# Layer 3's norm: the joining of the statistics on GpSimd, and the copy of x behind the root

## The chip, the core and the metric

The kernel runs on one core of a Trainium2 chip. The metric is the device time of one execution in microseconds (us), median of several runs. Engines are named as in the profile: PE (TensorE; PEld is its weight load), DVE (VectorE), ACT (ScalarE), POOL (GpSimd), SP (SyncE, which issues most DMAs).

## The reference

Four graph layers run one after the other over 16 batches of 512 nodes by 128 features. Each adds its result to x and is followed by a layer norm. The change is in the last layer (a graph attention with one head) and its norm:

```
m = mean(x); v = var(x); norm(x) = (x - m) / sqrt(v + eps)

Wh = x @ W;  s1 = Wh @ a1;  s2 = Wh @ a2
e = leaky_relu(s1[:, :, None] + s2[:, None, :])
e = where(adj == 0, -inf, e)
x = norm(x + softmax(e) @ Wh)
```

## The kernel before

Layer 3 works through 16 batches, b = 0 to 15. A batch is 512 nodes, held as four tiles of 128 nodes on the partitions. Every engine has its own hand-written list of items for one step; in `k:n` the item k works in step s on batch s − n. So PE, ACT and DVE work on several batches in one step, and each engine goes through its list strictly in order, waiting at semaphores.

- **PE** (L1447 to L1510) per step: `w0 q2 w1 q3 a3 i x a0 j a1 q0 q1 a2`. Item `x` transposes batch s from its copy `Xc` (L1458) and waits for that copy. `j` (L1477) makes the row terms s2 of the same batch, from the transposed x that ACT has copied out (`xTr`, L1322). `a0`, `a1`, `a2` (and `a3` one step later) multiply the exponentials `pr` by `Wh` (L1496) for batch s − 2. `w` (L1468), `q` (L1507, L1508) and `i` (L1484) are the other products.
- **DVE** per step: `m0 m1 d0 e0 e1 r0 m2 e2 e3 m3 r1 d1 c0 c1 r2 r3 b B`. The four `m` (L1377) take the row maxima of batch s and need its `j`. `e` (L1385) forms the scores of batch s − 1 and needs its `q`. For batch s − 2, `d` (L1401) and `r` (L1409) divide the product by its row sum and add x into the tile `rc`; `d1` needs `a3`. `b` takes the statistics of the norm (L142, four instructions: mean and sum of squares of the two halves of 128 features). `B` joins the halves (`bn_aggr`, L148, four instructions).
- **POOL** per step s, from s = 4 on (`pool_rest`, L1298): the copy of batch s into `Xc` (`pool_copy`, L1270 to L1275), then for batch s − 3 the root (L155 adds eps, L157 raises to −0.5), then the application, four instructions that write `rc` in place (L183). The first four copies and the norm of batch 0 are made ahead of that loop, so twelve copies (batches 4 to 15) are made in it.
- **SP** stores `rc` to memory when the application is done (L1243). Tiles `rc` exist twice, so `r` of batch b waits for the store of batch b − 2.

What sets the order around the change are these lists and the semaphores. The twelve copies stand in POOL's list in front of the root of batch s − 3, and thus right behind the application of batch s − 4. The norm of the last two batches ends differently: DVE applies it (`dve_last`, L1418 to L1437).

Of the kernel before, what the change touches and what calls it, by code (L numbers as in the profile page):

```python
# [23 lines left out]
ALU = mybir.AluOpType  # L24
# [3 lines left out]
P = 128  # L28
B, N, D = 16, 512, 128
NT = N // P  # L30
# [5 lines left out]
EPS = 1e-5  # L36
MASKED = -1.0e30
CREDIT = 2
# [3 lines left out]
def after(b, per, k=None):  # L42

    return (b + CREDIT) * per + (per if k is None else k)


def hold(eng, gate):


    eng.sem_inc(gate, 1)  # L50
# [136 lines left out]
def layer0(nc, m, ins, bank, L1):  # L187
# [3 lines left out]
    with ExitStack() as own:  # L191
# [112 lines left out]
        def order(text):  # L304
# [22 lines left out]
        }  # L327
        LAST = {
            "PE": order("#w0 #a0 p p p p #a1 #h0 p p p p #v0"),
# [814 lines left out]
def staged(text):  # L1144

    return [(word.split(":")[0], int(word.split(":")[1])) for word in text.split()]


def layer3(nc, own, m, bank, out, rl1_at, ready):
# [6 lines left out]
    def over(name, shape, dt=F32):  # L1156
        words = 1
        for n in shape[1:]:
            words *= n
        t = nc.alloc_sbuf_tensor_at(name, shape, dt, offset=at[0])  # L1160
        at[0] += -(-words * (2 if dt == BF16 else 4) // 32) * 32
        return t

    def sem(name):
        return own.enter_context(nc.semaphore("c_" + name))
# [11 lines left out]
    mx = [over(f"mx3{k}", [P, NT]) for k in range(2)]  # L1177
    em = [over(f"em{k}", [P, 2, NT]) for k in range(2)]
    rec = [over(f"rec3{k}", [P, NT]) for k in range(2)]
    at[0] = 205120  # L1180
    pr = [over(f"pr{k}", [P, NT, N]) for k in range(2)]
    norm = Norm(nc, own, m, "n3")
# [4 lines left out]
    x_f = sem("x_copied")  # L1187
# [9 lines left out]
    rcp = sem("reciprocal")  # L1197
    res = sem("residual")
    stored = [sem(f"stored{k}") for k in range(2)]
    last_eps, last_rstd, last_x, last_stored = (sem(f"last_{x}") for x in ("eps", "rstd", "applied", "stored"))  # L1200
    gate = sem("gate")
    LAST = B - 1
    out_bank = [bank[6], bank[7]]

    PE_ORDER = staged("w0:1 q2:2 w1:1 q3:2 a3:3 i:1 x:0 a0:2 j:0 a1:2 q0:1 q1:1 a2:2")
    ACT_ORDER = staged("L3:2 E0:2 W0:1 W1:1 E1:2 XR:0 G:1 L0:1 L1:1 X:0 L2:1")
    DVE_ORDER = staged("m0:0 m1:0 d0:2 e0:1 e1:1 r0:2 m2:0 e2:1 e3:1 m3:0 r1:2 d1:2 c0:0 c1:0 r2:2 r3:2 b:2 B:2")

    def is_batch(b, n):
        return isinstance(b, int) and b == n  # L1210
# [22 lines left out]
    third = Memory()  # L1233

    def sync(sp):
# [9 lines left out]

        pairs(sp, LAST - 1, 1, step)
        step(LAST - 1, 0, [True], LAST // 2)
        sp.wait_ge(last_x, 2)
# [12 lines left out]
    def pool_constants(pool):  # L1261
        pool.sem_inc(x_f, CREDIT)
        norm.credit_pool(pool)
        norm.credit_apply(pool)
        pool.wait_ge(*ready["O"])
        for n, ap in enumerate((onesb[:], Wh[0][:, :, 0:1], Wh[1][:, :, 0:1])):
            pool.memset(ap, 1.0).then_inc(const, 1)

    def pool_copy(pool, s, par, first=False):
        pool.wait_ge(x_ps, after(s - 2, 1))  # L1270
        pool.wait_ge(ready["X"], after(s, 4))
        if not first:
            pool.wait_ge(norm.s_x, after(s - 4, 4))
        hold(pool, gate)
        pool.tensor_copy(flat(Xf[par][:]), batch_flat(m.X, s)).then_inc(x_f, 1)  # L1275

    def pool_last_root(pool):
        rstd, aggr = norm.rstd[1], norm.aggr[1]
        pool.wait_ge(norm.s_x, after(LAST - 2, 4))
        for h in range(2):  # L1280
            two = slice(2 * h, 2 * h + 2)
            pool.wait_ge(norm.s_aggr, after(LAST, 4, 2 * h + 2))
            hold(pool, gate)
            pool.tensor_scalar(rstd[:, two], aggr[:, two, 1], EPS, 1.0, ALU.add, ALU.mult).then_inc(last_eps, 1)
            pool.wait_ge(last_eps, h + 1)
            pool.tensor_tensor(rstd[:, two], rstd[:, two], m.neg_half[:, 0:2], ALU.pow).then_inc(last_rstd, 1)

    def pool_norm(pool, b, par, copied):
        pool.wait_ge(x_f, after(copied, 1))
        if isinstance(b, int) and b == LAST:  # L1290
            pool_last_root(pool)
            return
        norm.root(pool, b + CREDIT, par)
        if isinstance(b, int) and b == LAST - 1:
            return
        norm.apply(pool, b + CREDIT, par, r[par], lambda k: r[par][:, k])

    def pool_rest(pool):  # L1298

        def step(s, par, alive, nth):  # L1300
            if alive[0]:
                pool_copy(pool, s, par)
            pool_norm(pool, s - 3, 1 - par, s if alive[0] else B - 1)

        pairs(pool, B, 4, step, first=4)

# [62 lines left out]
    def dve_items(dve):  # L1369

        def item(name, b, par, nth):
            what, k = name[0], int(name[1]) if name[-1].isdigit() else 0
            if what == "m":
                dve.wait_ge(s2_ps, after(b, 1))
                dve.wait_ge(s_mx, after(b, NT, k - 1))
                hold(dve, gate)
                dve.tensor_tensor_reduce(out=junk[k % 2][:], in0=s2_bank(b)[:], in1=m.mask_ij[:, k],  # L1377
                                         scale=1.0, scalar=3.0 * MASKED, op0=ALU.add, op1=ALU.max,
                                         accum_out=mx[par][:, k:k + 1]).then_inc(s_mx, 1)
            elif what == "e":  # L1380
                if k == 0:
                    dve.wait_ge(av, after(b - 2, NT))
                dve.wait_ge(relu, after(b, NT, k + 1))
                dve.wait_ge(r_ps, after(b, NT, k + 1))
                dve.scalar_tensor_tensor(out=pr[par][:, k], in0=bank[4 + k % 2][:],  # L1385
                                         scalar=Wh[par][:, k, S2_SLOPE:S2_SLOPE + 1], in1=rl[par][:, k],
                                         op0=ALU.add, op1=ALU.add).then_inc(e_s, 1)
            elif name == "c0":
                dve.wait_ge(s_mx, after(b, NT))
                dve.wait_ge(wh_c, after(b, 2))  # L1390
                dve.scalar_tensor_tensor(out=em[par][:, 0], in0=Wh[par][:, :, S1], scalar=SLOPE - 1.0, in1=mx[par][:],
                                         op0=ALU.mult, op1=ALU.subtract).then_inc(e_m, 1)
            elif name == "c1":
                dve.wait_ge(e_m, after(b, 2, 1))
                dve.wait_ge(d_g, after(b - 2, NT))
                dve.scalar_tensor_tensor(out=em[par][:, 1], in0=mx[par][:], scalar=-SLOPE, in1=em[par][:, 0],
                                         op0=ALU.mult, op1=ALU.min).then_inc(e_m, 1)
            elif what == "d":
                dve.wait_ge(av, after(b, NT, 2 * k + 2))
                dve.wait_ge(res, after(b - 2, NT))  # L1400
                dve.reciprocal(rec[par][:, 2 * k:2 * k + 2],  # L1401
                               out_bank[k][:, 0:2 * (D + 2)].rearrange("p (t d) -> p t d", t=2)[:, :, 0]
                               ).then_inc(rcp, 1)
            elif what == "r":
                h, t = divmod(k, 2)
                if t == 0:
                    dve.wait_ge(rcp, after(b, 2, h + 1))
                    dve.wait_ge(stored[par], (nth + 1) * 16)
                dve.scalar_tensor_tensor(out=r[par][:, k], in0=out_bank[h][:, t * (D + 2) + 1:t * (D + 2) + D + 1],  # L1409
                                         scalar=rec[par][:, k:k + 1], in1=tile_of(m.X, b, k),  # L1410
                                         op0=ALU.mult, op1=ALU.add).then_inc(res, 1)
            elif what == "b":
                dve.wait_ge(res, after(b, NT))
                norm.statistics(dve, b + CREDIT, par, r[par])
            elif what == "B":
                norm.aggregate(dve, b + CREDIT, par)

        return item  # L1418

# [101 lines left out]
def layers2_3(nc, m, bank, wide, out, L1):  # L1521
# [4 lines left out]
    with ExitStack() as own:  # L1526
# [3 lines left out]
        def sem(name):  # L1530
            return own.enter_context(nc.semaphore(name))
# [15 lines left out]
                 for h in range(2)] + late,  # L1547
# [8 lines left out]
        norm = Norm(nc, own, m, "n2")  # L1556

        bn = sem("bn_applied"); b_ps = sem("bn_turned"); res1 = sem("residual1")
        x_f = sem("x_in_place")
# [13 lines left out]
        gate = sem("gate")  # L1573
        agg = sem("bn2_aggregated"); root = sem("bn2_root"); aff = sem("bn2_factors")
        STACKED = 3 * 16
        third = layer3(nc, own, m, bank, out, qkT_at,
                       {"O": (bn, after(B - 1, 1)), "X": norm.s_x, "score banks": (s_mx, after(B - 1, TILES)),
                        "second wide": (t_exp, after(B - 1, EXPS)), "first two": (t_exp, after(B - 1, EXPS, EXPS - 1)),
                        "ring": ((rcp, after(B - 1, 1)), (o_n, after(B - 1, 1)))})
# [4 lines left out]
        DVE_ORDER = staged("ql:3 b:7 u3:4 kl:3 u0:3 R:0 c1:6 u1:3 B:0 c2:6 u2:3")  # L1584
# [73 lines left out]
        def _(pool):  # L1658
# [41 lines left out]
            third.pool_copy(pool, 2, 0, first=True)  # L1700
            third.pool_copy(pool, 3, 1, first=True)
            tail("r.15 g2.15", POOL_ORDER, work, None)
            third.pool_norm(pool, 0, 0, 3)
            third.pool_rest(pool)

        @block.scalar
# [311 lines left out]
```

## Time and profile before

| what | value |
|---|---|
| median of 3 runs | 933.6 us (933.47 to 933.91) |
| the profiled execution, device time | 933.39 us |
| its span, first to last instruction | 931.6 us |
| layer 3 in it | from about 795 us to the end |
| PE / DVE / ACT / POOL busy, 847.6 to 864.8 us (two steps, 17.2 us) | 16.57 / 15.83 / 14.35 / 9.94 us |

The difference between device time and span, 1.8 us, lies around the profile's first and last instruction. The views used are the table of busy time by stretch, the chain of waits (followed back from the last instruction and given in order of time), and the timeline (merged instructions in order of time; in brackets the engine's idle time just before, and what ended it).

### The profile page before, as it was taken

What the parts mean: (1) busy time and instruction counts of PE and PEld (TensorE: products, weight loads), DVE (VectorE), ACT (ScalarE), POOL (GpSimd) and SP (SyncE); (2) the same over time, 40 slices, a digit from 0 to 9 for tenths busy, and PEclk for the clock granted to TensorE, in tenths of its full rate; (3) what the DMA queues carried; (4) which work ended last, traced back from release to release, by engine and by line L of the source; (5) the groups of instructions that cost most, each with busy time, mean ns of one, the idle gap of its engine ahead of it and who ended that gap; (6) DMA issues with size and microseconds to landing.
All of it is one profiled execution on the core that took longest, in us unless ns stands there. A gap on an engine that the chain in (4) does not pass through costs nothing. (4 is left out here: it accounts for less than half of the span.)

```text
span 931.6 us, 20358 instructions
## 1 busy us (share of the span) xinstructions
PE 864.7 (93%) x6039; PEld 619.7 (67%) x6039; DVE 624.1 (67%) x1931; ACT 506.6 (54%) x903; POOL 404.0 (43%) x451
## 2 busy tenths in 40 slices
PE   6999999999999999977679999999999998999996
PEld 4799999999999998843344444444444444777775
DVE  4756645545545556467676887778876652899997
ACT  4332221211211236566457787888877667888884
POOL 4010211211111225300435788887887776456554
PEclk9999999999999999999979999999999999999999
DMA  9100000000010000000133443333433430010111
GB/s 253 35 9 15 13 12 12 24 12 13 23 30 4 13 1 0 0 0 1 34 70 69 87 102 86 68 78 81 99 82 69 87 86 1 13 34 23 34 34 45
DMA packets 34249, 40.82 MB, mean 44 GB/s; under 512 B 6673, under 2 KB 17553, under 8 KB 34193
## 3 DMA queue, kind: packets, MB, share of 16 engines
q1 hardware_dynamic: 32816, 39.87, 17.9%
q8 instruction: 28, 0.46, 0.2%
q10 hardware_dynamic: 1376, 0.27, 0.1%
q14 instruction: 29, 0.23, 0.1%
HBM read 6.43 MB, written 4.19 MB: 11 GB/s over the span
## 5 line engine op out<-in xcount | busy, mean ns | idle before, releaser
L1686 POOL TENSOR_TENSOR half_sum<-prob 128x1024 f32<-128x1024 f32 x64 | 151.4, 2378 | 21.3 <-PE bank L1950 18.4
L1761 ACT ACTIVATE prob<-wide 128x1024 f32<-128x1024 f32 x128 | 124.1, 1022 | 38.4 <-PE wide L1942 38.1
L460 ACT CAST yT<-wide 128x512 fp32r<-128x512 f32 x48 | 28.1, 589 | 190.8 <-PE wide L870 141.9
L1830 DVE CUSTOM_DVE_ANT_0 junk<-wide,mask_ij 128x512 bf16<-128x512 f32 x128 | 82.8, 684 | 51.2 <-PE bank L1922 50.7
L1938 PE MATMUL wide<-qk_st 128*128 128x512 f32 x256 | 84.5, 437 | 4.9 <-ACT prob L1761 3.3
L1830 DVE CUSTOM_DVE_ANT_0 junk<-bank,mask_ij 128x512 bf16<-128x512 f32 x128 | 83.0, 686 | 0.0
L553 POOL TENSOR_TENSOR Xr<-Xf,Xr 128x512 fp32r<-128x512 f32 x16 | 20.4, 1293 | 140.1 <-ACT Xr L455 139.9
L1496 PEld LDWEIGHTS bank<-Wh,pr 128*128 128x128 f32 x512 | 65.2, 191 | 14.0 <-ACT pr L1349 6.5
L1496 PE MATMUL bank<-Wh,pr 128*128 128x129 f32 x512 | 68.5, 278 | 4.8 <-ACT pr L1349 4.2
L59 PE MATMUL bank<-z,L3T_hi 128*128 128x256 f32 x256 | 72.4, 283 | 0.4 <-DVE z L678 0.4
L61 PE MATMUL bank<-z,L3T_lo 128*128 128x256 f32 x256 | 72.3, 283 | 0.0
L60 PE MATMUL bank<-z,L3T_hi 128*128 128x256 f32 x256 | 72.3, 282 | 0.0
L1938 PEld LDWEIGHTS wide<-qk_st 128*128 128x128 f32 x256 | 46.6, 194 | 32.4 <-DVE mx L1830 18.5
L155 POOL TENSOR_SCALAR n_rstd<-n_aggr 128x4 f32<-128x4 f32 x31 | 6.3, 204 | 129.1 <-DVE n_aggr L148 123.7
L1960 PE MATMUL bank<-prob,v 128*32 128x512 f32 x512 | 61.4, 598 | 0.2 <-ACT prob L1761 0.2
L664 DVE TENSOR_TENSOR yT<-wide,yT 128x512 fp32r<-128x512 f32 x48 | 32.9, 686 | 31.8 <-ACT yT L460 31.8
L687 DVE TENSOR_TENSOR zf<-bank,G 128x256 f32<-128x256 f32 x64 | 27.0, 421 | 34.6 <-PE bank L61 33.1
L59 PEld LDWEIGHTS bank<-z,L3T_hi 128*128 128x128 f32 x256 | 48.8, 191 | 2.0 <-DVE z L678 1.2
L60 PEld LDWEIGHTS bank<-z,L3T_hi 128*128 128x128 f32 x256 | 48.8, 191 | 0.4
L1922 PEld LDWEIGHTS wide<-qkT 32*128 32x128 f32 x128 | 12.3, 184 | 55.2 <-ACT prob L1761 29.2
L61 PEld LDWEIGHTS bank<-z,L3T_lo 128*128 128x128 f32 x256 | 48.9, 191 | 0.0
L558 POOL TENSOR_TENSOR Xa<-X,Xa 128x512 fp32r<-128x512 f32 x16 | 20.6, 1293 | 59.8 <-ACT Xa L429 59.8
(302 smaller groups left out, 2392.0 us busy)
## 6 DMA issues: line engine op xcount, KB each, us to landing
qk_st<-qkT SPq DMA_DIRECT2D x192, 128.0 KB, 2.4
out_dram<-rc SPq DMA_DIRECT2D x15, 256.0 KB, 2.3
Xf<-X SPq DMA_DIRECT2D x14, 256.0 KB, 2.3
A<-in_adj_dram SPq DMA_DIRECT2D x4, 256.0 KB, 5.0
qk_st<-neg_row SPq DMA_DIRECT2D x64, 2.0 KB
Xf<-in_x_dram SPq DMA_DIRECT2D x2, 256.0 KB, 7.0
mask_q<-mask_ji SPq DMA_DIRECT2D x16, 32.0 KB, 1.8
w<-in_L_gnn_W_dram SPq DMA_DIRECT2D x2, 128.0 KB, 2.2
```

The source lines that it names most:

```text
L59: pe.matmul(out, stat[0], mov[0], start=start, stop=False)
L60: pe.matmul(out, stat[0], mov[1], start=False, stop=False)
L61: return pe.matmul(out, stat[1], mov[0], start=False, stop=stop)
L460: act.copy(yT[bb][i][0][:], psum_y[i][:]).then_inc(y_hi, 1)
L664: dve.tensor_tensor(yT[bb][i][1][:], psum_y[i][:], yT[bb][i][0][:].bitcast(F32), ALU.subtract).then_inc(y_lo, 1)
L687: dve.tensor_tensor(zf[:, t], psum_h[k % 2][:, 0:GB * D], G[1 - par][:, 1 if k < NT else 0, t], ALU.add).then_inc(h_sb, 1)
L1496: last = pe.matmul(out_bank[h][:, t * (D + 2):t * (D + 2) + D + 1], pr[par][:, j, k * P:k * P + P], Wh[par][:, j, 0:D + 1], start=(j == 0) ...
L1686: pool.tensor_tensor(flat(half_sum[h][:]), flat(prob[bp][h][:, 0:2]), flat(prob[bp][h][:, 2:4]), ALU.add).then_inc(h_sum, 1)
L1761: act.activation(flat(prob[bp][h][:, 2 * half:2 * half + 2]), wide[half][:], ACT.Exp, scale=SCALE).then_inc(t_exp, 1)
L1830: dve.tensor_tensor_reduce(out=junk[h % 2][:], in0=ROWS[h][:], in1=m.mask_ij[:, i], scale=1.0, scalar=3.0 * MASKED, op0=ALU.add, op1=ALU.m ...
L1938: pe.matmul(bank[j][:], k_st[:, k, j * P:j * P + P], q_st[:, k], start=True, stop=True)
L1960: last = pe.matmul(ring["V0"][c, :], v[bp][:, k, c], prob[bp][h][:, k], start=(k == 0), stop=(k == NT - 1), skip_group_check=True)
```

## The change

POOL, not DVE, now joins the halves of the statistics. DVE's item `B` is gone. In its place POOL has `pool_root`: eight instructions on 128x4 operands (difference, sum and square of the means, sum of squares and their scaling), with semaphore waits on its own earlier results, and then the power as before. The copy of batch s, which stood in front of the root of batch s − 3, stands behind it and ahead of the application. The last batch keeps `bn_aggr` on DVE.

```diff
-    DVE_ORDER = staged("m0:0 ... c1:0 r2:2 r3:2 b:2 B:2")
+    DVE_ORDER = staged("m0:0 ... c1:0 r2:2 r3:2 b:2")
...
+    def pool_root(pool, b, par):
+        stats, aggr, rstd, w = norm.stats[par], norm.aggr[par], norm.rstd[par], terms[par]
+        means, sums = (stats[:, :, 1], stats[:, :, 4]), (stats[:, :, 2], stats[:, :, 5])
+        pool.wait_ge(norm.s_stats, after(b, 4))
+        pool.wait_ge(norm.s_x, after(b - 2, 4))
+        hold(pool, gate)
+        pool.tensor_tensor(w[:, 0], means[0], means[1], ALU.subtract).then_inc(s_joined, 1)
+        pool.tensor_tensor(w[:, 1], means[0], means[1], ALU.add).then_inc(s_joined, 1)
+        pool.tensor_tensor(w[:, 2], sums[0], sums[1], ALU.add).then_inc(s_joined, 1)
+        pool.wait_ge(s_joined, after(b, JOINED, 1))
+        pool.tensor_tensor(w[:, 3], w[:, 0], w[:, 0], ALU.mult).then_inc(s_joined, 1)
+        pool.wait_ge(s_joined, after(b, JOINED, 3))
+        hold(pool, gate)
+        pool.tensor_scalar(aggr[:, :, 0], w[:, 1], 0.5, 1.0, ALU.mult, ALU.mult).then_inc(s_joined, 1)
+        pool.tensor_scalar(w[:, 2], w[:, 2], 1.0 / D, EPS, ALU.mult, ALU.add).then_inc(s_joined, 1)
+        pool.wait_ge(s_joined, after(b, JOINED, 4))
+        hold(pool, gate)
+        pool.tensor_scalar(w[:, 3], w[:, 3], 0.25, 1.0, ALU.mult, ALU.mult).then_inc(s_joined, 1)
+        pool.wait_ge(s_joined, after(b, JOINED, 7))
+        pool.tensor_tensor(rstd[:], w[:, 2], w[:, 3], ALU.add).then_inc(norm.s_eps, 1)
+        pool.wait_ge(norm.s_eps, after(b, 1))
+        pool.tensor_tensor(rstd[:], rstd[:], m.neg_half[:, 0:NT], ALU.pow).then_inc(norm.s_rstd, 1)
...
-    def pool_norm(pool, b, par, copied):
-        pool.wait_ge(x_f, after(copied, 1))
+    def pool_norm(pool, b, par, copy=None):
...
-        norm.root(pool, b + CREDIT, par)
+        pool_root(pool, b, par)
+        if copy is not None:
+            pool_copy(pool, copy, 1 - par)
...
         def step(s, par, alive, nth):
-            if alive[0]:
-                pool_copy(pool, s, par)
-            pool_norm(pool, s - 3, 1 - par, s if alive[0] else B - 1)
+            pool_norm(pool, s - 3, 1 - par, s if alive[0] else None)
```

On POOL, before, from the application of batch 0 into the loop. The two copies `Xc_4721` and `Xc_4722` take turns (even and odd batches), as do `rc_4732` and `rc_4733`; ISA, REGISTER_ALU and branches are waits and bookkeeping:

```order
L183 TENSOR_SCALAR rc_4732<-rc_4732,n_aggr,n_rstd 128x128 x4
L94 UNCONDITIONAL_BRANCH
L94 ISA
L1271 ISA
L1273 ISA
L1275 ISA
L1275 COPY Xc_4721<-X 128x512
L1289 REGISTER_ALU
L152 ISA
L155 TENSOR_SCALAR n_rstd<-n_aggr 128x4
L157 TENSOR_TENSOR n_rstd<-n_rstd,neg_half 128x4
L183 TENSOR_SCALAR rc_4733<-rc_4733,n_aggr,n_rstd 128x128 x4
```

The copy of batch 4 is the loop's first work; the root of batch 1 comes behind it. On POOL, after, the end of the root of batch 1 in the same place (`terms_4744` holds the joined statistics of the odd batches; L1279 is the copy's new line):

```order
L1309 TENSOR_SCALAR terms_4744<-terms_4744 128x4
L1310 REGISTER_ALU
L1311 TENSOR_TENSOR n_rstd<-terms_4744 128x4
L1313 TENSOR_TENSOR n_rstd<-n_rstd,neg_half 128x4
L1274 REGISTER_ALU
L1275 ISA
L1277 ISA
L1279 ISA
L1279 COPY Xc_4721<-X 128x512
L183 TENSOR_SCALAR rc_4733<-rc_4733,n_aggr,n_rstd 128x128 x4
```

The same copy, of batch 4 into `Xc_4721`, now stands behind the root of batch 1, and ahead of its application. On DVE, before, the end of a step and the first row maximum of the next (`rc_4732` is an even batch, two behind):

```order
L1409 SCALAR_TENSOR_TENSOR rc_4732<-bank,rec_4741,X 128x128
L142 BN_STATS n_stats<-rc_4732 128x6 x4
L148 BN_AGGR n_aggr<-n_stats 128x2 x4
L1374 REGISTER_ALU
L1375 ISA
L1377 ISA junk_4728,mx_4738<-wide,mask_ij 128x512
```

And after:

```order
L1435 SCALAR_TENSOR_TENSOR rc_4732<-bank,rec_4741,X 128x128
L142 BN_STATS n_stats<-rc_4732 128x6 x4
L1400 REGISTER_ALU
L1401 ISA
L1403 ISA junk_4728,mx_4738<-wide,mask_ij 128x512
```

The `bn_aggr` row is gone, and the next step's first row maximum follows the statistics directly.

## Rows read from the trace of the kernel before

**Rows 1.** The page's first line.
```profile
span 931.6 us, 20358 instructions
```

**Rows 2.** Busy by stretch: stretch, length; PE, PEld, DVE, ACT, POOL; PEclk, DMA, GB/s.
```profile
847.60:864.80 17.20, 16.57 (x113) 12.78 (x112) 15.83 (x56) 14.35 (x29) 9.94 (x14) 1.00 0.11 31
```

**Rows 3.** Chain of waits, 844.7 to 862.8: start us, us, what.
```profile
844.89 0.65 PE wide L1458 x4
...
846.71 0.23 PE wide L1477
...
854.80 0.89 DVE n_stats L142 x4
...
856.43 0.21 POOL n_rstd L155
...
856.71 1.04 POOL n_rstd L157
...
861.36 0.60 POOL Xc L1275
...
862.09 0.65 PE wide L1458 x4
```

**Rows 4.** Timeline, POOL: small operations of layer 2's norm, first and last loop copy.
```profile
795.96 0.19 POOL L164 TENSOR_SCALAR n_rstd<-n_aggr 128x4 f32<-128x4 f32 x1 [2.06 <-DVE n_aggr L148]
796.24 0.20 POOL L165 TENSOR_SCALAR n_shift<-n_aggr 128x4 f32<-128x4 f32 x1
796.58 1.02 POOL L168 TENSOR_TENSOR n_rstd<-n_rstd,neg_half 128x4 f32<-128x4 f32 x1 [0.15 <-POOL n_shift L165]
...
809.47 0.61 POOL L1275 COPY Xc<-X 128x512 f32 x1 [0.25 <-POOL rc L183]
...
904.15 0.61 POOL L1275 COPY Xc<-X 128x512 f32 x1 [0.23 <-issue]
```

**Rows 5.** Timeline, DVE and PE: the pieces of one step of layer 3.
```profile
811.66 0.87 DVE L142 BATCH_NORM_STATS2 n_stats<-rc 128x6 f32<-128x128 f32 x4
...
821.03 1.05 PE L1496 MATMUL bank<-Wh,pr 128*128 128x129 f32 x8
...
826.33 1.02 PE L1484 MATMUL wide<-xTc,wB 128*128 128x512 f32 x2
...
847.94 0.69 DVE L1377 CUSTOM_DVE_ANT_0 junk<-wide,mask_ij 128x512 bf16<-128x512 f32 x1 [0.47 <-issue]
...
853.61 0.16 DVE L1401 RECIPROCAL rec<-bank 128x2 f32<-128x2 f32 x1
...
855.83 0.38 DVE L148 BATCH_NORM_AGGREGATE n_aggr<-n_stats 128x2 f32<-128x6 f32 x4 [0.16 <-DVE n_stats L142]
```

**Rows 6.** Timeline, PE: a wait late in layer 1, and one at layer 2's start.
```profile
407.21 9.23 PE L1138 MATMUL wide<-hf,W2T 128*128 128x512 f32 x17 [4.84 <-ACT hf L1096]
...
441.67 1.12 PE L1892 MATMUL bank<-ident,on 128*128 128x128 f32 x4 [5.06 <-ACT on L1725]
```

**Rows 7.** Busy by stretch after those waits, half microseconds; columns as Rows 2.
```profile
410.50:411.00 0.50, 0.50 (x2) 0.19 (x1) 0.10 (x1) 0.01 (x1) 0.00 (x0) 0.90 0.00 0
...
441.00:441.50 0.50, 0.00 (x0) 0.00 (x0) 0.00 (x0) 0.50 (x1) 0.00 (x0) 0.82 0.00 0
...
444.50:445.00 0.50, 0.50 (x3) 0.17 (x2) 0.35 (x5) 0.00 (x0) 0.00 (x0) 0.77 0.00 0
```

**Rows 8.** Timeline of the end, from the last transpose of x.
```profile
904.89 0.65 PE L1458 MATMUL wide<-ident,Xc 128*128 128x128 f32 x4
...
914.82 0.87 DVE L142 BATCH_NORM_STATS2 n_stats<-rc 128x6 f32<-128x128 f32 x4
...
917.93 3.13 POOL L183 TENSOR_SCALAR rc<-rc,n_aggr,n_rstd 128x128 f32<-128x128 f32 x4 [0.21 <-POOL n_rstd L157]
```

**Rows 9.** Chain of waits at the end: start us, us, what.
```profile
921.30 2.29 DMA out_dram<-rc
...
923.67 0.62 DVE rc L1409 x2
```

More of the change, by code:

```diff
@@ L1179, in layer3 @@
     rec = [over(f"rec3{k}", [P, NT]) for k in range(2)]
+    terms = [over(f"terms3{k}", [P, 4, NT]) for k in range(2)]
     at[0] = 205120
@@ L1199, in layer3 @@
     stored = [sem(f"stored{k}") for k in range(2)]
+    s_joined = sem("halves_joined")
     last_eps, last_rstd, last_x, last_stored = (sem(f"last_{x}") for x in ("eps", "rstd", "applied", "stored"))
@@ L1202, in layer3 @@
     LAST = B - 1
+    JOINED = 7
     out_bank = [bank[6], bank[7]]
@@ L1206, in layer3 @@
     ACT_ORDER = staged("L3:2 E0:2 W0:1 W1:1 E1:2 XR:0 G:1 L0:1 L1:1 X:0 L2:1")
-    DVE_ORDER = staged("m0:0 m1:0 d0:2 e0:1 e1:1 r0:2 m2:0 e2:1 e3:1 m3:0 r1:2 d1:2 c0:0 c1:0 r2:2 r3:2 b:2 B:2")
+    DVE_ORDER = staged("m0:0 m1:0 d0:2 e0:1 e1:1 r0:2 m2:0 e2:1 e3:1 m3:0 r1:2 d1:2 c0:0 c1:0 r2:2 r3:2 b:2")
     def is_batch(b, n):
@@ L1264, in pool_constants @@
         norm.credit_apply(pool)
+        pool.sem_inc(s_joined, CREDIT * JOINED)
         pool.wait_ge(*ready["O"])
@@ L1281, in pool_last_root @@
             two = slice(2 * h, 2 * h + 2)
-            pool.wait_ge(norm.s_aggr, after(LAST, 4, 2 * h + 2))
+            pool.wait_ge(norm.s_aggr, CREDIT * 4 + 2 * h + 2)
             hold(pool, gate)
@@ L1414, in item @@
                 norm.statistics(dve, b + CREDIT, par, r[par])
-            elif what == "B":
-                norm.aggregate(dve, b + CREDIT, par)
         return item
@@ L1702, in _ @@
             tail("r.15 g2.15", POOL_ORDER, work, None)
-            third.pool_norm(pool, 0, 0, 3)
+            third.pool_norm(pool, 0, 0)
             third.pool_rest(pool)
```

## The prediction

> **What bounds the kernel now.** I read the table of busy time by stretch first. In two steps of layer 3 (17.2 us) PE is busy for 16.57 us and DVE for 15.83 [rows 2]. So no engine has much room, and busy time alone does not say which wait ends last. The chain of waits does [rows 3]. It leaves DVE after the statistics (854.80, for 0.89: ends 855.69), goes through the joining, the root and the application on POOL, and then to the copy of x (861.36). From there it goes to PE's transpose of that copy (862.09), and through PE and DVE to the next statistics of the chain. The reader is to see that a copy of x is a link of the chain, and why: POOL's list has it behind an application.
>
> Batch numbers make this a cycle. The transpose of batch s waits for its copy, which stands behind the application of batch s − 4, which needs the statistics of batch s − 4. The transpose of batch s in turn leads, within its step, to the statistics of batch s − 2. So the cycle spans two batches. Its pieces from the chain: transpose 844.89 to the end of statistics 855.69, 10.80 us; from there to the end of the copy 861.96, 6.27; to the next transpose 862.09, 0.13. The sum is 17.20, the length of two steps, and so 8.6 us for a batch.
>
> **The change, and what it does to that cycle.** The order lists shown with the change decide the forecast. In them the copy of batch s stands behind the root of batch s − 3, no longer ahead of it. The application is out of the way of the copy, but the copy now needs the statistics of batch s − 3, and the transpose of batch s leads to the statistics of batch s − 2. So the cycle spans one batch, and everything in it is paid in each step: statistics, root, copy, transpose, PE's step, and statistics again. DVE cannot fill the gap, since its next item is the row maximum of batch s, which needs that transpose. PE cannot either: `x` stands in front of `a0` in its list.
>
> Each link in turn:
>
> 1. *Statistics to root on POOL.* From the end of the joining (855.83 + 0.38) to the root's first operation (856.43) it took 0.22 [rows 3, 5]. I take the same from the statistics.
> 2. *The eight new operations.* The trace has no such group, but POOL's root of layer 2 works on operands of the same size: 0.28 us from start to start (795.96 to 796.24), and 0.34 where waits stand between (796.24 to 796.58) [rows 4]. The eps and the power of today's root are 0.28 apart (856.43 to 856.71) [rows 3]. In the new root two operations have a wait and a `hold` ahead of them. So it is six steps of 0.28 and two of 0.34, 2.36 us to the start of the power. Bounds: eight bare lengths of 0.20 give 1.6, eight times 0.34 give 2.7. I stay near the upper one, since spacing and not length counts.
> 3. *The power*, 1.04 [rows 3].
> 4. *The copy*: 0.25 of gap and 0.60 [rows 4, 3]; then 0.13 to PE, as above.
>
> From the end of the statistics to the transpose this is 0.22 + 2.36 + 1.04 + 0.25 + 0.60 + 0.13 = 4.60 us.
>
> 5. *Transpose to the end of the next statistics.* Before it is 10.80 us, of which DVE loses some by being late for its first row maximum (847.94), 1.0 us after `j` was done (846.71 + 0.23) [rows 3, 5]. In the changed kernel DVE waits for `j`, and begins at about 0.12 behind it, 2.2 us after the transpose starts. From the first row maximum to `d1` it worked 5.67 us (847.94 to 853.61), so `d1` is at 7.9. PE must have ended `a3` by then: `a1` starts with the end of `j`, at 2.05, and an unhindered PE came from `a1` to the end of `a3` in 5.30 us (821.03 to 826.33) [rows 5], so at 7.35. `d1` to the end of the statistics took 2.08 (853.61 to 855.69), the sum is 10.0. I add 0.1 for the `e` that come just at the end of their `q`: 10.1, with bounds of 9.9 and the 10.80 of before.
>
> So a step takes 14.7 us, if TensorE's clock stays at 2.4 GHz.
>
> 6. *The clock.* In such a step PE ends `i` at about 8.3 us and has nothing more to do until 14.7, a pause of 6.4 us. The trace has two comparable waits of PE, 4.84 us before 407.21 and 5.06 us before 441.67 [rows 6]. In the second the granted clock fell to half (1.2 GHz) before the wait ended: 0.82 in the half microsecond from 441.0, so at about 441.3. It was back at about 444.7 (0.77 in the half microsecond from 444.5), and after the first wait at about 410.6 (0.90 in that from 410.5) [rows 7]. So work ran at half speed for 3.1 and 3.4 us and lost half of that, 1.5 to 1.7 us. The pause here is longer, so a part of the stretch at half speed may lie in the pause and cost nothing: with half of it there, the loss is about 0.85. I take 1.3 in every step, with bounds of 0 and 1.7. All of it is on the path, since it delays `j`, `q` and `a3` alike. By the Trainium skill (TensorE: Matmul & The Clock Gate, section on HAM oscillation), a loop of short bursts of matmuls with long waits between them starts every burst at the lower clock; both waits agree, and by that rule the first rival below falls away.
>
> A step is then 14.7 + 1.3 = 16.0 us, where it was 8.6.
>
> *How many steps.* Twelve copies are made in the loop, 809.47 the first and 904.15 the last [rows 4]. Batch 4 must wait for the statistics of batch 1, which end at about 812.5 (811.66 + 0.87) [rows 5]; its transpose is at 817.1. Eleven steps later batch 15 is transposed at 817.1 + 11 × 16.0 = 993.1, in place of 904.89 [rows 8].
>
> *The end.* From that transpose to the end of the statistics of batch 13 it is 10.1 + 1.3 = 11.4. Then comes the part that carries the root's length: before, from the end of those statistics (915.69) to `r` of the last batch (923.67) it took 7.98 us, through root, application (3.13) and the store of batch 13, whose tile the last batch needs [rows 8, 9]. There the new root takes 2.36 where the wait, the joining and the eps took 0.16 + 0.38 + 0.28 = 0.82 [rows 5, 3]: 9.5. From `r` to the span's end nothing changes, 7.9 [rows 1, 9]. The span ends at 993.1 + 11.4 + 9.5 + 7.9 = 1021.9 us. With the 1.8 us between span and device time this is **1024 us**. The profiled execution (933.39) lies 0.2 under the median, which I neglect.
>
> *What is removed.* DVE's joining, 0.38 + 0.16 of gap per batch [rows 5], sits where DVE now waits for POOL, so it gives nothing beyond link 1. Stores and SP's queue see later applications, but `r` needs a store of two batches before, a whole step away: nothing.
>
> On POOL's operations the Trainium skill (GPSIMD Engine Reference, section 4.1, Engine selection) says that work on two inputs takes about twice VectorE's time there. The rows show 0.16 for a small DVE operation and 0.20 for one on POOL, so less than that. By the rule the five two-input operations would take 0.32 each, 0.6 us more in a step, and the time would be about 1031.
>
> **Rivals.**
>
> *The clock does not fall* in the pauses. Then each step is 14.7: 817.1 + 161.7 + 27.5 = 1006.3, and the time is 1008 us. Against it: both waits of rows 6.
>
> *The clock stays down through the burst.* PE's 7.35 us to `a3` double, the step becomes about 22 us, and the time about 1096. Against it: in both cases it came back within 3.4 us of work.
>
> *Not slower at all: the copy is not of the batch I think.* Were the copy in the loop one batch further ahead, the cycle would span two batches, at 4.6 + 10.8 = 15.4 us without the application. DVE would decide from there, at 17.2 less two joinings with their gaps (1.08), 16.1 for two batches. Over 12 batches this saves 6.5 us: 927 us. The deciding point is which batch's copy stands behind the root of batch 1 in the loop. The list has `Xc_4721` there, the even tile, as its first copy, and batches 0 to 3 were copied before the loop: batch 4. I leave it a small chance, together with a reader's error of the batch in PE's list.
>
> **How the numbers follow.** The forecast (a one-batch cycle with a falling clock) has 0.75, the steady clock 0.14, the clock that stays down 0.05, the two-batch cycle 0.03; 0.03 is for a slowdown of another size. The forecast's own bounds: root and copy −0.76 to +0.34 per step, link 5 −0.2 to +0.7, clock −1.3 to +0.4. Not all fall together; half of the sum over 12 steps is some 14 us down and 9 us up. The range takes in the steady clock, and reaches up to where all upper ends together would lie (12 × 1.44 = 17 us up): 1004 to 1041. A measurement of this kernel can tell about 0.2% from no change; slower by more has 0.97, faster 0.02, the same 0.01.
>
> **What would show it.** Right: copies of `Xc` about 16 us apart, each right behind a power; PE waiting some 6 us for `Xc` in each step, and a granted clock under 1 in layer 3; DVE's first row maximum no longer right behind the statistics, but some 7 us later. The eight operations show link 2 directly. Wrong: copies still 8.6 us apart, or a PE whose wait is for something else than `Xc`.

## The result and the profile after

The changed kernel takes 1021.8 us (median of 6 runs, 1020.31 to 1023.14), the kernel before beside it 933.5 (6 runs, 932.89 to 935.22): 1.094 times as long, 95% interval 1.093 to 1.096. The forecast was 1024. The profiled execution took 1020.31 us.

The page of the kernel after, first its span, then the busy tenths of PE and DVE and the granted TensorE clock in 40 slices of 25.5 us each:

```profile
span 1018.3 us, 20439 instructions
...
PE   6999999999999998966899999999998675665756
...
DVE  4756654555455555758688778777653753645546
...
PEclk9999999999999999997999999999999987878779
```

The span is 86.7 us longer than in [rows 1]. All of it lies in the last fifth, which is layer 3: there PE is busy for some six tenths of a slice, DVE for some five, and the clock is down in part of each slice. Where the time stands in a step, the timeline shows (start us, us, engine, line, operation, out<-in; in brackets the idle time before, and what ended it). L1298 to L1313 are the new root, L1279 is the copy of x, L1482 PE's item `x`:

```profile
893.49 1.11 PE L1482 MATMUL wide<-ident,Xc 128*128 128x128 f32 x4 [5.70 <-POOL Xc L1279]
...
904.91 0.88 DVE L142 BATCH_NORM_STATS2 n_stats<-rc 128x6 f32<-128x128 f32 x4
906.06 0.20 POOL L1298 TENSOR_TENSOR terms<-n_stats 128x4 f32<-128x4 f32 x1 [9.58 <-DVE n_stats L142]
906.21 0.20 POOL L1299 TENSOR_TENSOR terms<-n_stats 128x4 f32<-128x4 f32 x1
906.36 0.20 POOL L1300 TENSOR_TENSOR terms<-n_stats 128x4 f32<-128x4 f32 x1
906.51 0.20 POOL L1302 TENSOR_TENSOR terms<-terms 128x4 f32<-128x4 f32 x1
906.76 0.20 POOL L1305 TENSOR_SCALAR n_aggr<-terms 128x4 f32<-128x4 f32 x1
907.04 0.19 POOL L1306 TENSOR_SCALAR terms<-terms 128x4 f32<-128x4 f32 x1
907.32 0.19 POOL L1309 TENSOR_SCALAR terms<-terms 128x4 f32<-128x4 f32 x1
907.59 0.20 POOL L1311 TENSOR_TENSOR n_rstd<-terms 128x4 f32<-128x4 f32 x1
907.87 1.03 POOL L1313 TENSOR_TENSOR n_rstd<-n_rstd,neg_half 128x4 f32<-128x4 f32 x1
908.86 0.61 POOL L1279 COPY Xc<-X 128x512 f32 x1
909.46 3.13 POOL L183 TENSOR_SCALAR rc<-rc,n_aggr,n_rstd 128x128 f32<-128x128 f32 x4
...
909.61 1.11 PE L1482 MATMUL wide<-ident,Xc 128*128 128x128 f32 x4 [5.78 <-POOL Xc L1279]
```

This is one whole turn of the cycle that the prediction wrote down: transpose, statistics, root, copy, transpose. It takes 909.61 − 893.49 = 16.12 us. In [rows 3] the same round trip carries two batches in 17.20 us, and here it carries one. The twelve copies of the loop stand at 813.54 to 988.31, so a step is 174.77 / 11 = 15.89 us on average (8.6 before; 16.0 forecast).

Who waits for whom from 815 to 1000 us (engine, line, waited for: us in total, times, longest us):

```profile
POOL terms L1298 <- DVE n_stats L142: 102.9, 11, 10.1
DVE junk L1403 <- PE wide L1501: 88.2, 12, 7.4
ACT xTr L1348 <- PE wide L1482: 72.7, 12, 6.1
...
PE wide L1482 <- POOL Xc L1279: 63.1, 11, 5.8
```

All four engines wait once in each step, each for the one ahead of it in the cycle: POOL for the statistics, PE for the copy, ACT for PE's transpose, DVE's first row maximum for `j` (L1501), some 7.35 us (88.2 / 12). The lists that overlapped have become a chain.

Busy by stretch (columns as Rows 2), for the whole loop and at the two ends of one dip of the clock:

```profile
815.00:1000.00 185.00, 119.66 (x646) 99.38 (x657) 91.98 (x283) 86.43 (x168) 70.03 (x157) 0.79 0.06 17
...
891.50:892.00 0.50, 0.00 (x0) 0.00 (x0) 0.00 (x0) 0.00 (x0) 0.42 (x2) 0.71 0.00 0
...
893.50:894.00 0.50, 0.50 (x3) 0.50 (x4) 0.00 (x0) 0.00 (x0) 0.50 (x1) 0.50 0.00 0
...
898.50:899.00 0.50, 0.39 (x2) 0.20 (x2) 0.17 (x1) 0.50 (x2) 0.00 (x0) 0.97 0.11 29
```

Over the loop the granted clock is 0.79 of full, where a stretch of two steps before had 1.00 [rows 2]. It falls to half, 1.2 GHz, in the pause (0.71 over the half microsecond from 891.5, so at about 891.7), PE starts again at 893.49 at half speed, and 2.4 GHz is back at about 898.5. The transposes show it too: four take 1.11 us here, 0.65 before [rows 3].

The end of the chain of waits (start us, us, what), which answers [rows 8, 9]:

```profile
989.05 1.11 PE wide L1482 x4
...
1000.68 0.67 DVE n_stats L142 x3
...
1004.62 3.15 POOL rc L183 x4
...
1007.98 2.29 DMA out_dram<-rc
1010.37 0.62 DVE rc L1435 x2
```

### The profile page after: what moved, and what is told of

It reads as the page before. It is cut to its first block and busy times, and to the rows that moved or that the text cites. A ratio compares the mean times of both kernels' runs of the same rounds, so it can differ in the third digit from the quotient of the medians.

```text
span 1018.3 us, 20439 instructions
## 1 busy us (share of the span) xinstructions
PE 883.4 (87%) x6021; PEld 642.1 (63%) x6039; DVE 621.4 (61%) x1871; ACT 507.1 (50%) x903; POOL 421.9 (41%) x556
## 3 DMA queue, kind: packets, MB, share of 16 engines
q1 hardware_dynamic: 32816, 39.87, 16.4%
## 5 line engine op out<-in xcount | busy, mean ns | idle before, releaser
L1854 DVE CUSTOM_DVE_ANT_0 junk<-wide,mask_ij 128x512 bf16<-128x512 f32 x128 | 82.8, 684 | 51.3 <-PE bank L1946 50.7
L1403 DVE CUSTOM_DVE_ANT_0 junk<-wide,mask_ij 128x512 bf16<-128x512 f32 x60 | 39.9, 684 | 88.9 <-PE wide L1501 88.8
L1520 PEld LDWEIGHTS bank<-Wh,pr 128*128 128x128 f32 x512 | 83.6, 238 | 10.4 <-ACT pr L1375 3.7
L1520 PE MATMUL bank<-Wh,pr 128*128 128x129 f32 x512 | 84.7, 322 | 3.0 <-ACT pr L1375 2.4
L1482 PE MATMUL wide<-ident,Xc 128*128 128x128 f32 x60 | 15.2, 402 | 69.6 <-POOL Xc L1279 68.9
L1482 PEld LDWEIGHTS wide<-ident,Xc 128*128 128x128 f32 x60 | 9.9, 202 | 81.0 <-issue 81.0
L1298 POOL TENSOR_TENSOR terms<-n_stats 128x4 f32<-128x4 f32 x15 | 3.0, 203 | 121.2 <-DVE n_stats L142 121.2
L1411 DVE SCALAR_TENSOR_TENSOR pr<-bank,Wh,rl 128x512 f32<-128x512 f32 x64 | 46.1, 746 | 7.7 <-PE bank L1532 6.3
```

Of the source, the lines that this page charges most:

```text
L1482: last = pe.transpose(x_bank(b)[:, t * P:t * P + P], Xf[par][:, t], m.ident[:])
L1520: last = pe.matmul(out_bank[h][:, t * (D + 2):t * (D + 2) + D + 1], pr[par][:, j, k * P:k * P + P], Wh[par][:, j, 0:D + 1], start=(j == 0) ...
L1854: dve.tensor_tensor_reduce(out=junk[h % 2][:], in0=ROWS[h][:], in1=m.mask_ij[:, i], scale=1.0, scalar=3.0 * MASKED, op0=ALU.add, op1=ALU.m ...
```

## The experiments

Theory A is the prediction's: the copy of batch s behind the root of batch s − 3 makes the cycle one batch long; the eight operations on POOL matter only because they lie in it. Theory B puts the loss on POOL's joining itself. The first two kernels part them. The medians of before beside them are 934.0 us (19 runs) for e1, e2, e3 and e5, and 933.5 (13 runs) for the rest.

**e1: the joining on POOL, the copy ahead of the root again** (against after)

```diff
-        pool_root(pool, b, par)
         if copy is not None:
             pool_copy(pool, copy, 1 - par)
+        pool_root(pool, b, par)
```

> The changed kernel with the copy of batch s put back ahead of the root of batch s − 3; the joining stays on GpSimd. Theory A (the copy's place makes the cycle one batch long): the cycle spans two batches again. Its POOL part, from the end of the statistics to the transpose, is 0.27 + 1.81 (the new root as measured after) + 1.03 + 0.22 + 3.13 + 0.25 + 0.60 + 0.13 = 7.44 us, where it was 6.40; the other part was 10.80 and can lose up to 0.54, since DVE no longer joins in between. So 17.7 to 18.2 us for two batches, where it was 17.2: some 3 to 7 us over before, 937 to 941 us. Theory B (the chain of eight small operations on GpSimd is what costs): still 1010 us or more.

It took 936.7 us (8 runs, 935.49 to 937.87), 1.003 times before (95% interval 1.002 to 1.004, as in the brackets behind each ratio below). One call moved takes 85 of the 88 us away, so B falls. The 2.7 us that are left are the joining's own. Timeline of e1, lines numbered as in after:

```profile
839.38 0.87 DVE L142 BATCH_NORM_STATS2 n_stats<-rc 128x6 f32<-128x128 f32 x4
...
847.66 0.65 PE L1482 MATMUL wide<-ident,Xc 128*128 128x128 f32 x4 [0.95 <-POOL Xc L1279]
...
849.93 0.69 DVE L1403 CUSTOM_DVE_ANT_0 junk<-wide,mask_ij 128x512 bf16<-128x512 f32 x1 [1.27 <-PE wide L1501]
...
856.96 0.87 DVE L142 BATCH_NORM_STATS2 n_stats<-rc 128x6 f32<-128x128 f32 x4
```

The two-batch cycle can be read off: end of the statistics (840.25) to the transpose (847.66) is 7.41 us, where it was 6.40 in [rows 3] (855.69 to 862.09). Transpose to the end of the next statistics in the chain (857.83) is 10.17, where it was 10.80, since DVE is now early and waits 1.27 us for `j`. The sum is 17.58 for two batches, and the copies are 17.57 apart. So the joining's price here is 0.37 us for two batches, small because DVE's slack pays most of it.

**e2: the joining on DVE, only the copy moved behind the root** (against before; the wait for `x_f` goes with it, as in the change)

```diff
-            if alive[0]:
-                pool_copy(pool, s, par)
-            pool_norm(pool, s - 3, 1 - par, s if alive[0] else B - 1)
+            pool_norm(pool, s - 3, 1 - par, s if alive[0] else None)
...
         norm.root(pool, b + CREDIT, par)
+        if copy is not None:
+            pool_copy(pool, copy, 1 - par)
...
```

> The kernel before with only the copy moved behind the root; the joining stays on DVE. Theory A: the one-batch cycle is there without the joining on GpSimd. From the statistics to the transpose: 0.16 + 0.38 + 0.22 + 0.28 + 1.0 + 0.61 + 0.13 = 2.8 us, where the changed kernel shows 3.82, so 1.0 us less in each of 12 steps: about 1009 us, 1003 to 1015. Theory B: near before, 934 to 940 us.

It took 1006.1 us (2 runs, 1005.28 and 1006.92), 1.078 times before (1.076 to 1.079). The copy's place alone costs 72 us. Before, e1, e2 and after are thus the four combinations of two places of the copy and two engines for the joining, and only the copy's place makes a loss of this size. Timeline of e2 (PE's lines have numbers one lower than before, so L1457 is item `x`):

```profile
841.61 0.87 DVE L142 BATCH_NORM_STATS2 n_stats<-rc 128x6 f32<-128x128 f32 x4
...
845.31 0.66 PE L1457 MATMUL wide<-ident,Xc 128*128 128x128 f32 x4 [4.78 <-POOL Xc L1275]
```

With the joining on DVE the way from the end of the statistics to the transpose is 2.83 us (842.48 to 845.31), 0.99 less than after (below), and a step is 14.60 (copies from 815.07 to 975.63). The last 16 us of after's loss are thus the price of the joining on POOL once it lies in a one-batch cycle. In e1 the same eight operations cost 2.7. Of the 1.29 us between the two steps (15.89 and 14.60) 0.99 is the longer way itself; the other 0.3 is, by my estimate, the clock: with the 10.04 of e5 below for the rest of the step, it costs 14.60 − 2.83 − 10.04 = 1.73 us a step in e2, and 2.10 in after.

**e5: after, with PE kept busy in the pause** (against after; the products go to a bank that is written again before it is read)

```diff
+                if not isinstance(b, int) or b >= 4:
+                    pe.wait_ge(s_mx, after(b - 1, NT))
+                    for _ in range(22):
+                        pe.matmul(bank[2][:], m.identb[:], m.mask_ji[:, 0], start=True, stop=True)
```

> The changed kernel with 22 matmuls of 128x512 (bf16, some 4.7 us at 2.4 GHz) ahead of the transpose of batches 4 to 15, written to the bank of the row terms, which the following product overwrites. They fill the pause in which PE waits for the copy (5.7 us). Theory A with the clock as a term: the granted clock stays at 1.0 in layer 3, a step falls from 15.9 to 3.82 + 10.0 = 13.8 us, and the time by 12 times 2.1 us to about 997 us (992 to 1003). If the clock costs nothing on the path: 1019 to 1024 us.

It took 999.1 us (2 runs, 998.64 and 999.59): 22.7 us less than after, by work that the result doesn't need. Busy by stretch in e5 (columns as Rows 2):

```profile
818.00:970.00 152.00, 140.15 (x835) 94.40 (x851) 83.91 (x264) 78.24 (x154) 68.10 (x155) 1.00 0.07 19
```

and its timeline (L1486 is item `x` there):

```profile
841.90 0.20 POOL L1298 TENSOR_TENSOR terms<-n_stats 128x4 f32<-128x4 f32 x1 [7.25 <-DVE n_stats L142]
...
844.70 0.61 POOL L1279 COPY Xc<-X 128x512 f32 x1
...
845.44 0.65 PE L1486 MATMUL wide<-ident,Xc 128*128 128x128 f32 x4 [1.02 <-POOL Xc L1279]
...
854.61 0.87 DVE L142 BATCH_NORM_STATS2 n_stats<-rc 128x6 f32<-128x128 f32 x4
```

The granted clock is 1.00 over the loop. PE still waits for `Xc`, so the filling delays nothing, and the cycle stays: copies are 13.79 us apart (817.12 to 968.79). What is gone is only the half-speed work. The clock's price in after is 15.89 − 13.79 = 2.10 us in a step. From the transpose (845.44) to the end of the statistics (854.61 + 0.87 = 855.48) it is 10.04 us.

**e3: after, with the copy of batch s + 1 in that place** (against after; the waits and the ends of the loop follow the new batch number)

```diff
-            pool.wait_ge(norm.s_x, after(s - 4, 4))
+            pool.wait_ge(norm.s_x, after(s - 5, 4))
...
-            pool_copy(pool, copy, 1 - par)
+            pool_copy(pool, copy, par)
...
-            pool_norm(pool, s - 3, 1 - par, s if alive[0] else None)
+            pool_norm(pool, s - 3, 1 - par, None if isinstance(s, int) and s + 1 >= B else s + 1)
...
-        pairs(pool, B, 4, step, first=4)
+        pairs(pool, B, 4, step, first=4, loop_to=B - 2)
...
-            third.pool_norm(pool, 0, 0)
+            third.pool_norm(pool, 0, 0, 4)
```

> The changed kernel with the copy one batch further ahead: batch s + 1 between the root and the application of batch s − 3 (batch 4 in the norm of batch 0). Theory A: the cycle spans two batches at 3.82 + 10.8 = 14.6 us or less and no longer decides; VectorE does, at 0.54 us less per batch than before. 13 batches give 7.0 us, and the longer root of the end takes back about 1.0 us: 926 to 929 us. Theory B: the eight operations still stand in the way, 950 us or more.

It took 933.2 us (12 runs, 931.27 to 935.8), 1.000 times before (0.999 to 1.001). The root, the copy and the application stand in after's order; only the copy's batch is another, and all of the loss is gone. This is the plainest evidence for A. But the further 4 to 7 us that I expected, those of the third rival, did not come. The chain of waits of e3 says why (start us, us, what):

```profile
845.22 1.15 PE bank L1520 x8
...
851.01 0.91 PE bank L1520 x8
...
852.56 1.08 ACT pr L1375
853.68 1.16 PE bank L1520 x8
```

and two rows of its timeline:

```profile
846.92 0.69 DVE L1403 CUSTOM_DVE_ANT_0 junk<-wide,mask_ij 128x512 bf16<-128x512 f32 x1 [0.76 <-PE wide L1501]
...
852.02 0.66 ACT L1357 COPY Wh<-wide 128x262 f32<-128x262 f32 x2 [1.31 <-PE bank L1520]
```

Neither POOL nor DVE is in it. PE works from `a0` (845.22) to the end of `a3` (851.92); ACT's copy of `Wh` (L1357) waits for that; ACT's exponential (L1375) is behind it in ACT's list; the next `a0` (853.68) waits for the exponential. That is 8.46 us for one batch. DVE, which I had named as what decides at 8.05 (16.1 for two), waits 0.76 us in the step. The copies of e3 are 8.50 us apart on average, those of before 8.61. What e3 gains by that in eleven steps, 1.2 us, the longer root takes back at the end: from the end of the statistics of batch 13 there (914.27) to `r` of the last batch (923.36) it is 9.1 us, where it was 7.98.

**e4: before, with the copy one batch ahead, the joining on DVE** (against before: the edits of e3 around `norm.root`)

```diff
-            pool_norm(pool, s - 3, 1 - par, s if alive[0] else B - 1)
+            pool_norm(pool, s - 3, 1 - par, None if isinstance(s, int) and s + 1 >= B else s + 1)
...
         norm.root(pool, b + CREDIT, par)
+        if copy is not None:
+            pool_copy(pool, copy, par)
...
```

> The kernel before (DVE joins the halves) with the copy of batch s + 1 between the root and the application of batch s − 3. With the copy off the chain, what holds the step is the next loop behind it. If that is the loop of TensorE and ScalarE which the run with the copy one batch ahead shows (8.53 us from one a0 to the next, through W and E1), the joining on either engine makes no difference: 932 to 934 us. If VectorE's own work still binds, the 0.54 us of joining per batch show: 3 us or more over that run, 935 us or more.

It took 933.5 us (10 runs), 1.000 times before (0.999 to 1.001), as e3. With the copy ahead it makes no difference to the time on which engine the halves are joined. The chain of waits of e4 (L1495 is `a0` here, L1348 ACT's exponential):

```profile
845.17 1.15 PE bank L1495 x8
...
852.68 1.08 ACT pr L1348
853.80 1.16 PE bank L1495 x8
```

Between 840 and 880 us this chain holds PE and ACT alone, as in e3, and yet the copies are 8.60 us apart (805.46 to 900.11), as before (8.61). So with the joining on DVE the loop of PE and ACT is as long as POOL's cycle, and taking the copy out of that cycle gains nothing. The 0.1 us that e3 has less per step goes with the joining off DVE; why the loop is shorter there, no run tells.

**e6, e6b and e7: the lists rearranged, to break the loop of PE and ACT** (e6 against e3; e6b is e6 with DVE's old list; e7 has the e6 lists in e4, with the joining on DVE)

```diff
-    PE_ORDER = staged("... i:1 x:0 a0:2 j:0 a1:2 q0:1 ...")
-    ACT_ORDER = staged("L3:2 E0:2 W0:1 W1:1 E1:2 XR:0 ...")
-    DVE_ORDER = staged("... r1:2 d1:2 c0:0 c1:0 r2:2 r3:2 b:2")
+    PE_ORDER = staged("... i:1 a0:2 x:0 a1:2 j:0 q0:1 ...")
+    ACT_ORDER = staged("L3:2 E0:2 E1:2 W0:1 W1:1 XR:0 ...")
+    DVE_ORDER = staged("... r1:2 d1:2 r2:2 r3:2 b:2 c0:0 c1:0")
```

> The kernel with the copy one batch ahead, and three lists changed so that the loop found there is opened: ScalarE makes E1 ahead of W0 and W1, PE does a0 ahead of x and a1 ahead of j, DVE does c0 and c1 behind the statistics. Between a3 and a0 there passed 1.86 us, of which PE worked 0.9 for i and 0.65 for x. If that loop was the bound, PE goes from i to a0 without waiting and a step falls from 8.53 to 8.0 to 8.2 us: 12 steps give 4 to 6 us, 927 to 930 us. If something else held the step, 932 to 935 us, as without the new lists.

> As the run with three changed lists, but DVE's list left as it was, so that c0 and c1 stand ahead of the last two residuals and the statistics. W comes about 0.9 us later than before, and DVE waits for it at c0. If DVE has that much room, the time is that of the three lists (927 to 930 us); if not, the gain is lost again: 931 to 936 us.

> The three changed lists with the joining on DVE (B behind c1), the copy one batch ahead. This is the case in which DVE's joining can be seen, if VectorE comes to bind: then 0.38 us more per batch than with the joining on GpSimd, 4 to 5 us over that run. If PE binds, both are the same within 1 us.

All three missed: 942.7 us (ratio 1.010, 1.008 to 1.011), 944.4 (1.012, 1.010 to 1.014) and 942.6 (1.010, 1.008 to 1.012). Timeline of e6:

```profile
856.82 1.06 ACT L1375 ACTIVATE pr<-pr 128x1024 f32<-128x1024 f32 x1 [0.96 <-DVE pr L1411]
...
857.93 1.16 PE L1520 MATMUL bank<-Wh,pr 128*128 128x129 f32 x8 [0.25 <-ACT pr L1375]
...
860.28 0.49 PE L1501 MATMUL wide<-xTr,wB 128*128 128x512 f32 x1
861.45 0.39 PE L1531 MATMUL bank<-mask_ji,identb 128*128 128x512 bf16 x1 [0.68 <-ACT dg L1370]
```

The wait for `Wh` is gone, and a longer loop stands in its place. PE's `j` now starts 2.35 us behind `a0` (857.93 to 860.28), in e3 0.9. DVE waits for it, and so forms its scores later; ACT's last exponential waits 0.96 us for those scores, and `a0` for the exponential. A step is 9.27 us (`a0` at 848.66 and 857.93). I moved `x` off the way of `a0` and thereby put DVE's whole list behind `j`. That reading rests on these rows; e6b shows that DVE's move is not the cause, and no run makes the moves in PE's and in ACT's list apart. e7, at 942.6 beside e6's 942.7, shows that the joining's engine plays no part in the time here either.

## Why the prediction was right, step by step

**The cycle** (from two batches to one) is shown: e1 and e3 change only the copy's place or its batch, and the loss goes. The batch numbers read in the order lists carried the whole forecast; no busy share in the profile of before said anything of it.

**The links** of one step, the measured ones from the turn of after shown above:

| link | forecast us | measured us |
|---|---|---|
| 1, statistics to root | 0.22 | 0.27 (905.79 to 906.06) |
| 2, eight operations | 2.36 | 1.81 (906.06 to 907.87) |
| 3 and the gap, power to copy | 1.04 + 0.25 | 0.99 (907.87 to 908.86) |
| 4, copy, and on to PE | 0.60 + 0.13 | 0.75 (908.86 to 909.61) |
| statistics to transpose, sum | 4.60 | 3.82 |
| 5, transpose to statistics, full clock | 10.1 | 10.0 (e5) |
| 6, clock | 1.3 | 2.1 (after less e5) |
| step | 16.0 | 15.89 |

Link 2 was sized too high, though it stayed inside its bounds (1.6 to 2.7). I took 0.28 from start to start, and the rows that I took it from all begin with an operation on one input [rows 3, 4]. The first four of the new root have two inputs and start 0.15 apart (906.06, 906.21, 906.36, 906.51); from there on it is 0.25 to 0.28. Waits alone do not make that difference: L1302 has one ahead of it and starts 0.15 behind L1300, while none stands between L1305 and L1306, which start 0.28 apart. Whether the kind of operation makes it, no run tells by itself. Nor is there a gap ahead of the copy, which starts (908.86) before the power's end (908.90). The gap of 0.25 was taken from a copy that stood behind an application [rows 4]. With links 1 and 4 that is 0.78 too much.

Link 5 held, in e5 to 0.1 us and in e1 as well (10.17). DVE's lateness of before did leave the path, as the step assumed.

Link 6 was sized too low, and beyond its upper bound (1.7). I let half of the low stretch fall into the pause. In the turn shown the clock fell only 1.8 us before PE started again (891.7, 893.49), and 5.0 us of work ran at half speed, which would be 2.5 us if all of it were on the path; the mean over the steps is 2.1. The two waits of [rows 6, 7] had 3.1 and 3.4 us of such work; in after it differs from step to step (the rows at the end of this text have 3.1 to 5.9). The Trainium skill (TensorE: Matmul & The Clock Gate, section on HAM oscillation) says that short bursts of matmuls with long waits between them start each burst at the lower clock; this trace agrees, with 0.50 in the half microsecond from 893.5 and in the first microsecond behind each of the loop's twelve transposes, though a burst here lasts 10.3 us (893.49 to 903.82) and so is longer than the wait.

So a step that was right to 0.1 us had two errors in it, −0.78 and +0.8, which happen to cancel. The mechanism was read; that the sum is so close is luck.

**Beginning and end.** The transpose of batch 4 came at 814.29, not 817.1. The statistics of batch 1 end 2.1 us earlier than taken (809.57 + 0.88, in place of 812.53): layer 3 began earlier in this execution (its first transpose at 778.00, before 779.58) and DVE's joining is gone; the rest is link 2. Eleven steps on, batch 15 is transposed at 989.05 (forecast 993.1). From there to the end of the statistics of batch 13 it is 12.3 us (989.05 to 1001.35; 11.4 forecast, the clock again), from there to `r` 9.0 (1010.37; 9.5 forecast, the root again), and from `r` to the span's end 7.9, as forecast. So the span ends 3.6 us before the forecast's 1021.9: 2.8 from the beginning and 1.2 from the eleven steps, less 0.4 given back at the end.

**The price of POOL's operations.** Operations with two inputs take 0.20 us, those with one 0.19 to 0.20 (906.06, 907.04). DVE's own operation on two tiles of that size takes 0.15 in the same turn:

```profile
903.80 0.15 DVE L1417 SCALAR_TENSOR_TENSOR em<-Wh,mx 128x4 f32<-128x4 f32 x1
```

The Trainium skill (GPSIMD Engine Reference, section 4.1, Engine selection) puts two-input work at about twice VectorE's time; on 128x4 operands the rows show 1.3 times, and the 1031 us worked out by it did not come. (The 0.16 doubled there was that of a reciprocal, an operation on one input of 128x2 [rows 5].)

**The rivals.** "The clock does not fall" was put at 1008 us. e5, in which it is kept from falling, took 999, since the way from the statistics to the transpose was 0.8 us a step shorter than that sum has it. "The clock stays down" did not come: it returned within the burst. "The copy is one batch further ahead" was put at 927, and e3, which is that kernel, took 933.2: the step that failed there is that DVE would decide next. The loop of PE and ACT, at 8.46 us, was not in my list of cycles, though its wait was in the trace of before: ACT's copy of `Wh` waited for PE there 11 times between 815 and 905 us, 8.9 us in total.

## What to carry to other kernels

Where in-order lists on several engines work on different batches, write down for each wait which batch it needs and which batch it releases: a cycle's cost in a step is its length over the number of batches that it spans, and moving one instruction past another can change that number from two to one, which no busy share shows. Taking a link out of the cycle that binds gains only the distance to the next cycle, so all of them have to be counted first; here the next one was as long (8.60 us in e4, 8.61 before). Work that is free while its engine waits for someone else is paid in full once that engine's list is a link of a one-batch cycle: the same eight operations cost 2.7 us in one order and 16, with the clock's part, in the other.

## What was not expected of the hardware

- The first small operations of the root on POOL start 0.15 us apart though each is shown as 0.20 long, and the copy starts 0.04 us before the end of the power ahead of it (rows of after, 906.06 to 908.86). Further on in the same root they are 0.25 to 0.28 apart. (The profile gives spans on POOL as rough.)
- Work that the result doesn't need made a kernel faster: 22 matmuls in each pause of PE kept the granted clock at 1.00 and took 22.7 us off 1021.8.
- The step of after isn't steady: copies are 16.4, 15.1, 16.0, 16.6, 15.1, 16.1 us apart and so on, while those of e5 are a steady 13.8. The clock makes the difference: it falls at another point of the pause in each step, and so leaves another amount of work at half speed. Busy by stretch in after, 9 us from each of three transposes in a row (columns as Rows 2):

```profile
861.80:870.80 9.00, 8.78 (x45) 7.69 (x47) 4.46 (x11) 5.61 (x11) 3.00 (x4) 0.67 0.10 29
878.40:887.40 9.00, 8.94 (x54) 7.75 (x55) 5.46 (x13) 5.97 (x13) 2.98 (x4) 0.83 0.10 29
893.49:902.49 9.00, 8.85 (x50) 8.06 (x52) 4.72 (x12) 5.60 (x11) 2.99 (x4) 0.72 0.10 29
```

Clocks of 0.67, 0.83 and 0.72 over 9 us mean 5.9, 3.1 and 5.0 us at half speed. These steps, from transpose to transpose, take 16.60, 15.09 and 16.12 us, which is 2.81, 1.30 and 2.33 more than the 13.79 of e5: some 0.45 us lost for each microsecond at half speed.
